# A sandwich transformer on one core: the third stage's ways laid out on a table with one hop between engines for each round

## What is computed

```python
# L2 attention: 16 heads of 8 channels, causal softmax over the 256 tokens, out projection
# L2 MLP
h = gelu(x @ w1 + b1, approximate=False); return h @ w2 + b2
# L3
xm = resid_mix_m[0] * x + resid_mix_m[1] * x0
vg = rms_norm(xm) @ in_proj_w; value, gate = vg[..., :256], vg[..., 256:]
value = silu(causal_conv(value, conv_w, 4) + conv_b)
y = selective_scan(value, A, xm @ B_proj_w, xm @ C_proj_w, dt, 64) + D_param * value
xm = xm + mamba_scale * (y * silu(gate) @ out_proj_w)
xm = xm + m_mlp_scale * mlp(rms_norm(xm), m_fc_w, m_proj_w)      # mlp: square(relu(n @ fc)) @ proj
xa = resid_mix_a[0] * xm + resid_mix_a[1] * x0
q, k, v = rms_norm(xa) @ q_w, ... @ k_w, ... @ v_w                # 16 heads, 4 key heads, 8 channels
q, k = apply_rope(rms_norm(q), cos, sin) * q_gain, apply_rope(rms_norm(k), cos, sin)
xa = xa + attn_scale * (causal_softmax_attention(q, k, v) @ o_w)
xa = xa + a_mlp_scale * mlp(rms_norm(xa), a_fc_w, a_proj_w)
```

## Time and profile before

| what | us |
|---|---|
| median of 2 runs (4128.28 to 4131.64) | 4129.96 |
| the profiled execution | 4135.6 |
| its span, first to last instruction | 4134.0 |
| third stage in it (2059.5 to 3815.0) | 1755.5 |
| PE busy in the span | 3113.1 (75%) |
| DVE busy | 2393.2 (58%) |
| ACT busy | 1826.8 (44%) |
| POOL busy | 622.3 (15%) |
| mean granted clock of PE | 0.832 |

### The profile page before, as it was taken

How to read it: one execution, slowest core, us unless ns; L and a number is a source line. 1 busy time by engine, 2 the same in 40 slices (tenths; PEclk the granted TensorE clock), 3 DMA queues, 4 the chain that set the end, 5 groups by cost and what they waited for, 6 DMA issues and landing times.

```text
span 4134.0 us, 76115 instructions
## 1 busy us (share of the span) xinstructions
PE 3113.1 (75%) x31950; PEld 2440.1 (59%) x31950; DVE 2393.2 (58%) x6438; ACT 1826.8 (44%) x3876; POOL 622.3 (15%) x651
## 2 busy tenths in 40 slices
PE   6788887788887688787666785866878659466795
PEld 3566665466665577687544673755747548354465
DVE  4655555664555798989742655656456455533327
ACT  3555555456554777777412332422424224212322
POOL 1210011110101222222200113021010220300000
PEclk7888988889988789899856897988879879766797
DMA  2000000000000000000000000000000000000000
GB/s 79 1 1 1 1 2 1 1 1 1 1 1 37 11 8 6 9 6 4 11 1 1 1 2 0 2 1 1 3 1 2 1 1 2 1 1 30 12 1 21
DMA packets 13542, 27.99 MB, mean 7 GB/s; under 512 B 784, under 2 KB 9232, under 8 KB 12688
## 3 DMA queue, kind: packets, MB, share of 16 engines
q1 hardware_dynamic: 13200, 23.12, 1.6%
HBM read 21.02 MB, written 2.10 MB: 6 GB/s over the span
## 4 chain that ended last, share of the span: by engine, by line
PE 51%; DVE 32%; ACT 10%; POOL 3%; issue 3%; DMA 0%; SPq 0%; DVEq 0%; POOLq 0%; ACTq 0%
PE ps L374 6%; PE ps L383 5%; DVE LN L2000 4%; PE ps L436 4%; PE ps L348 3%; PE ps L1878 3%; PE ps L525 3%; PE ps L1358 3%; POOL wAB L1755 3%; DVE LN L541 3%; DVE RS L289 2%; DVE LN L2013 2%; ACT LN L320 2%; DVE LN L310 2%; PE ps L443 1%
## 5 line engine op out<-in xcount | busy, mean ns | idle before, releaser
L356 ACT COPY LN<-ps 128x512 f32<-128x512 f32 (+4 forms) x592 | 303.5, 546 | 883.1 <-PE ps L348 474.7
L335 POOL TENSOR_TENSOR RS<-RS,MISC 128x4 f32<-128x4 f32 x216 | 220.4, 1021 | 2144.3 <-DVE RS L301 1687.2
L348 PE MATMUL ps<-cons,LN 128*128 128x128 f32 x672 | 149.4, 369 | 458.9 <-DVE LN L308 183.1
L541 DVE TENSOR_REDUCE LN<-ps 128x6 f32<-128x768 f32 x256 | 244.3, 956 | 288.9 <-PE ps L426 148.8
L348 PEld LDWEIGHTS ps<-cons,LN 128*128 128x128 f32 x672 | 103.2, 186 | 490.8 <-DVE LN L308 191.0
L436 PE MATMUL ps<-LN 32*128 32x256 f32 x1024 | 209.5, 488 | 105.1 <-DVE LN L541 39.6
L374 PE MATMUL ps<-LN,wAB 128*128 128x512 f32 x384 | 229.0, 727 | 16.9 <-ACT LN L393 8.5
L2000 DVE TENSOR_TENSOR LN<-LN 128x1024 f32<-128x1024 f32 (+2 forms) x192 | 220.3, 1147 | 27.8 <-ACT LN L356 16.9
L439 PE MATMUL ps<-LN 32*128 32x256 f32 x1024 | 210.1, 491 | 26.4 <-DVE LN L541 23.4
L687 DVE TENSOR_REDUCE M<-ps 128x12 f32<-128x1536 f32 x64 | 112.4, 1756 | 175.0 <-PE ps L426 174.9
L1878 PE MATMUL ps<-LN,wAB 128*128 128x128 f32 x1024 | 150.9, 310 | 74.2 <-ACT LN L356 73.7
(11 more groups left out here) (352 smaller groups left out, 7860.1 us busy)
## 6 DMA issues: line engine op xcount, KB each, us to landing
wAB<-wb SPq DMA_DIRECT2D x16, 256.0 KB, 2.7
LN<-wd SPq DMA_DIRECT2D x8, 512.0 KB, 6.7
...
```

The source lines that it names most:

```text
L335: pool.e.tensor_tensor(c.r[:, 40:44], c.r[:, 36:40], mhalf, ALU.pow).then_inc(*c.G.inc((k, "rstd")))
L348: ins = pe.e.transpose(ps[:, n * 128:(n + 1) * 128], src[:, n, :], ident)
L356: act.e.copy(dst, ps).then_inc(*c.A.inc(named(k, done)))
L541: return dve.e.tensor_reduce(cols[:, 2 - 2 * h:4 - 2 * h, :, q.at], src, X_AX, ALU.max, negate=True)
```

## The change

The parts of a lane's way get a table of rounds. A new class `Pace` counts rounds, and `p.to(n)` yields until round n; all engines of a part use the same numbers. Each step of DVE, POOL, PE and ACT gets a round of its own, so that what one engine makes in a round another takes in the next one. `mid` goes from 53 to 68 rounds (20 ahead of the scan, 32 in it, 16 behind), `l3_out` from 6 to 11, `l2_in` from 4 to 5, and couple 1 starts in round 60, not 52. A couple then has 8 + 50 + 71 + 50 + 19 + 50 + 71 + 50 + 14 = 383 rounds, and the stage 443. `dve_norm` is split (`dve_apply`), `dve_residual` applies a norm and adds, `pe_up` and `pe_down` are the two halves of `pe_mlp`. The instructions, their shapes and their number are the same, apart from the activation table loads, which follow the order of ACT's functions: there are 4 more of them in the third stage. The scan's own code and `attend` are not touched.

```diff
 LW = 8192
-LAG3, START3 = 3, (0, 52)
-ROUNDS3 = {"l2_in": 4, "mid": 53, "l3_out": 6}
+LAG3, START3 = 3, (0, 60)
+ROUNDS3 = {"l2_in": 5, "mid": 68, "l3_out": 11}
 START1 = (0, 4, 9, 13)
...
+
+    def __init__(self):
+        self.now = 0
+
+    def to(self, rnd):
+        while self.now < rnd:
+            self.now += 1
+            yield
...
         def pe_mid(pe, c, g):
-            v, attended = views23(c), couple_signals[c.n // 2][1]
+            v, attended, p = views23(c), couple_signals[c.n // 2][1], Pace()
             XT = v["XT"]
             k = (("l2", g // 4), c.n)
             pe.wait_ge(attended, (("l2", g // 4), 2 * (c.n % 2) + 1, "on"))
             pe_tok(pe, c, k, wv("l2o"), XT, 0, c.A, "y")
-            yield
-            yield
+            yield from p.to(5)
             k = (g, "l2f")
             pe.wait_ge(c.D, (k, "normed", 3))
             pe_tr4(pe, c, k, v["XN"], 0, c.A)
-            yield
+            yield from p.to(6)
             pe.wait_ge(c.A, (k, "xT"))
-            yield from pe_mlp(pe, c, k, XT, wv("l2w1"), 4, w3("l2w2"), v["h3"], c.D, c.A)
-            yield
-            yield
+            pe_up(pe, c, k, XT, wv("l2w1"), (0, 1), c.A)
+            yield from p.to(7)
+            pe_up(pe, c, k, XT, wv("l2w1"), (2, 3), c.A)
+            yield from p.to(8)
+            pe_down(pe, c, k, w3("l2w2"), v["h3"], c.A)
+            yield from p.to(13)
             k = (g, "l3m")
             pe.wait_ge(c.D, (k, "mixed"))
             pe_tr4(pe, c, k, v["Z"], 0, c.A)
-            yield
...
                         *c.P.inc((k, part, n)))
-                yield
+                yield from p.to(17 if part == "val" else 20)
             for b in range(2):
                 yield from pe_scan(pe, c, (g, "scan", b), b, v, (g, "l3n"), (g, "l3m"))
-            yield from pe_relu_mlp(pe, c, (g, "mm"), v, "mfc", "mpj")
-            yield
+            p.now = 52
+            yield from pe_relu_mlp(pe, c, (g, "mm"), v, "mfc", "mpj", p)
+            yield from p.to(61)
             k = (("l3", g // 4), c.n)
...
                 ins.then_inc(*c.P.inc((k, g2, "qkv_pe")))
-            yield
-            yield
-            yield
+            yield from p.to(67)
             pe.wait_ge(c.D, (k, "roped"))
             pe_tr4(pe, c, k, v["QK"][:, :, 0:128], 0, c.D, "qa")
             pe_tr4(pe, c, k, v["KR"], 1, c.A, "ka")
...
+        def pe_up(pe, c, k, xT, w1, js, by):
+            for j in js:
+                ps = c.bank(pe, j % 2, by, (k, "h", j))
+                pe.e.matmul(ps[:, :], w1[:, j * 128:(j + 1) * 128], xT, start=True, stop=True).then_inc(
+                    *c.P.inc((k, "up", j)))
+
+        def pe_down(pe, c, k, w2, h3, by):
...
+        def pe_relu_mlp(pe, c, k, v, fc, pj, p):
+            r = p.now
+            yield from p.to(r + 2)
             pe.wait_ge(c.D, (k, "normed", 3))
             pe_tr4(pe, c, k, v["YN"], 0, c.A)
-            yield
+            yield from p.to(r + 3)
...
             pe.wait_ge(c.A, (k, "xT"))
-            yield from pe_mlp(pe, c, k, v["XT"], wv(fc), 4, w3(pj), v["h3"], c.D, c.D)
+            pe_up(pe, c, k, v["XT"], wv(fc), (0, 1), c.D)
+            yield from p.to(r + 4)
+            pe_up(pe, c, k, v["XT"], wv(fc), (2, 3), c.D)
+            yield from p.to(r + 5)
+            pe_down(pe, c, k, w3(pj), v["h3"], c.D)

...
+        def dve_relu_mlp(dve, c, k, v, rep, p):
+            r = p.now
+            dve_stats(dve, c, k, v["Z"], rms=True, eps=EPS)
+            yield from p.to(r + 1)
+            dve_apply(dve, c, k, v["Z"], v["YN"], rms=True)
+            for i in range(2):
+                yield from p.to(r + 3 + i)
+                for j in (2 * i, 2 * i + 1):
+                    dve.wait_ge(c.A, (k, "relu", j))
+                    dve.e.scalar_tensor_tensor(v["h3"][:, j, :], c.ps[j % 2][:, :], 0.0, v["h3"][:, j, :], ALU.max,
+                                               ALU.mult).then_inc(*c.D.inc((k, "h", j)))
+            yield from p.to(r + 6)
             scaled(dve, c, k, "sum", "y", v["Z"], rep, v["tmp"])
...
         def dve_mid(dve, c, g):
-            v = views23(c)
+            v, p = views23(c), Pace()
             X, XN, O4, Z, YN, QK = XG[g], v["XN"], v["O4"], v["Z"], v["YN"], v["QK"]
-            k = (("l2", g // 4), c.n)
-            dve.wait_ge(c.A, (k, "y"))
-            yield from dve_post(dve, c, (g, "l2ap"), X, O4)
+            yield from p.to(1)
+            dve.wait_ge(c.A, ((("l2", g // 4), c.n), "y"))
+            dve_stats(dve, c, (g, "l2ap"), O4)
+            yield from p.to(2)
+            dve_residual(dve, c, (g, "l2ap"), X, O4)
+            yield from p.to(3)
+            dve_stats(dve, c, (g, "l2f"), X)
+            yield from p.to(4)
+            dve_apply(dve, c, (g, "l2f"), X, XN)
+            yield from p.to(9)
             k = (g, "l2f")
-            yield from dve_norm(dve, c, k, X, XN)
-            yield
-            yield
-            yield
             dve.wait_dma(got_ve)
             dve.wait_ge(c.P, (k, "sum"))
             dve.e.tensor_tensor(O4, v4(c.ps[0]), rep4(wv("l2b2")), ALU.add).then_inc(*c.D.inc((k, "y")))
-            yield from dve_post(dve, c, (g, "l2fp"), X, O4)
-            yield from dve_norm(dve, c, (g, "l3x"), X, XN)
+            dve_stats(dve, c, (g, "l2fp"), O4)
+            yield from p.to(10)
+            dve_residual(dve, c, (g, "l2fp"), X, O4)
+            yield from p.to(11)
+            dve_stats(dve, c, (g, "l3x"), X)
+            yield from p.to(12)
+            dve_apply(dve, c, (g, "l3x"), X, XN)
             dve.wait_ge(c.D)
             dve.wait_ge(DD[LANES], "rm")
             dve.e.tensor_tensor(Z, XN, rep4(wv("rm0")), ALU.mult).then_inc(*c.D.inc(((g, "l3m"), "mixed")))
+            yield from p.to(13)
             k = (g, "l3n")
-            yield from dve_norm(dve, c, k, Z, YN, rms=True, eps=EPS)
-            yield
+            dve_stats(dve, c, k, Z, rms=True, eps=EPS)
+            yield from p.to(14)
+            dve_apply(dve, c, k, Z, YN, rms=True)
             cw = wv("convw")
             for n in range(2):
+                yield from p.to(17 + n)
...
-                yield
+            yield from p.to(20)
             for b in range(2):
                 yield from dve_scan(dve, c, (g, "scan", b), b, v, k)
-            yield from dve_relu_mlp(dve, c, (g, "mm"), v, wv("mmsc"))
+            p.now = 52
+            yield from dve_relu_mlp(dve, c, (g, "mm"), v, wv("mmsc"), p)
             dve.wait_ge(c.D)
             mixed(dve, c, (g, "am"), Z, Z, wv("ra0"), XN, wv("ra1"), v["tmp"])
+            yield from p.to(59)
             k = (("l3", g // 4), c.n)
-            yield from dve_norm(dve, c, k, Z, YN, rms=True, eps=EPS)
-            yield
-            yield
+            dve_stats(dve, c, k, Z, rms=True, eps=EPS)
+            yield from p.to(60)
+            dve_apply(dve, c, k, Z, YN, rms=True)
+            yield from p.to(63)
             rb, sq, un = v["rb"], v["sq"], v["un"]
             dve.wait_ge(c.A, (k, 1, "qkv"))
...
-            yield
+            yield from p.to(64)
+            r4 = rb.rearrange("p (t c) -> p t c", c=20)
             dve.wait_ge(c.G, (k, "rms"))
...
         def dve_l3_out(dve, c, g):
-            v = views23(c)
+            v, p = views23(c), Pace()
+            yield from p.to(1)
             scaled(dve, c, (("l3", g // 4), c.n), "y_pe", "y", v["Z"], wv("asc"), v["tmp"])
-            yield from dve_relu_mlp(dve, c, (g, "am"), v, wv("amsc"))
-            yield from dve_post(dve, c, (g, "l3p"), XG[g], v["Z"])
-            yield
+            yield from p.to(2)
+            yield from dve_relu_mlp(dve, c, (g, "am"), v, wv("amsc"), p)
+            yield from p.to(9)
+            dve_stats(dve, c, (g, "l3p"), v["Z"])
+            yield from p.to(10)
+            dve_residual(dve, c, (g, "l3p"), XG[g], v["Z"])
+            yield from p.to(11)
...
+
+        def dve_residual(dve, c, k, X, Y):
+            dve_apply(dve, c, k, Y, Y)
+            dve.wait_ge(c.D)
+            dve.e.tensor_tensor(X, X, Y, ALU.add).then_inc(*c.D.inc((k, "x")))
```

More of the change, by code:

```diff
@@ L1740, in pool_mid @@
-            yield from pool_norm(pool, c, (g, "l3n"))
-            v = views23(c)
+            v, p = views23(c), Pace()
+            for r, name in ((1, "l2ap"), (3, "l2f"), (9, "l2fp"), (11, "l3x"), (13, "l3n")):
+                yield from p.to(r)
+                pool_rstd(pool, c, (g, name))
             pool.wait_ge(c.D, ((g, "l3m"), "mixed"))
             pool.e.memset(v["XV"], 0.0).then_inc(*c.G.inc((g, "scan", "zeros")))
-            yield from idle(3)
+            yield from p.to(20)
@@ L1760, in pool_l3_out @@
[L1760 to L1762 removed]
+            p = Pace()
+            yield from p.to(2)
+            pool_rstd(pool, c, (g, "am"))
+            yield from p.to(9)
+            pool_rstd(pool, c, (g, "l3p"))
+            yield from p.to(11)
         XTA, YA = LN[:, 0:4096], LN[:, 8192:12288].rearrange("p (b m e) -> p b m e", b=16, m=2)
```

165 lines of the change are left out of this document (83 added, 82 removed).

## The result

The changed kernel takes 4011.7 us (median of 2 runs, 4011.3 to 4012.1) where the kernel before took 4130.0: a ratio of 0.9714, 95% interval 0.9672 to 0.9755, 118 us or 2.9% faster. Its profiled span is 4009.8 us, 124 less than before. It lies in the forecast range (3945 to 4150) and on the forecast side; the forecast was 4066, so the gain was nearly twice the forecast one. It doesn't lie in the main case's own range (4020 to 4110), and the likeliest outcome by the chances was a difference of under 2% (0.56, against 0.38 for a gain of over 2%).

The account below looks back on a forecast made before the run. The prediction took scans as PE-bound and the third stage's rest as bound by waits. Rest 788 less 855.4, plus 4 elsewhere, gave -63.7 from 4135.6: 4071.9, or 4066 after the 5.6 median offset; range 3945 to 4150.

Parts of the forecast that it names:

- main case: Whole kernel: the summed forecast of 4066 us, chance 0.53, with its own range of 4020 to 4110.
- Bound: Third stage outside scans and attention alone: waits bind, no engine; PE's 350 us for normed input are all its idle time.
- the rest: Third stage's seven stretches with steps ahead of or behind the scan, `l3_out` or `l2_in`: from 855.4 to 788 us.
- Known stretches: Third stage's scans, attention beside attention, last attention and opening: priced by known rounds, together +4 us.
- The power: Head norms' power on POOL, 13.1 us, eight times: DVE's wait grows from 64.8 to 82 us, counted in full.
- The price of a round: 178 new rounds outside scans and attention alone: 706 us without the head norms' power, 4.0 each.
- packed rival: Same stretches: uneven rounds average out between queues, PE 87% busy, 659 us, total 3937; chance 0.25.
- The toll: Same stretches: each round costs its hops and loop whatever stands in it, 4.98 us, total 4166; chance 0.15.
- Table loads: ACT in the third stage: four more loads of 1.28 us, taken as nothing, 5 us kept for the range.
- It doesn't do what it says: Third stage: relu MLPs keep relu and square in one round, power one round long; little moves, 4110 to 4140; chance 0.07.

Follow-up runs that it names:

- the padded kernel: Kernel before with its old steps, empty rounds added to give each part its length after the change, couple 1 starting in round 60: 4191.3 us, ratio 1.0160.
- the kernel with the narrow power: Changed kernel with POOL's power of the head norms on 4 of its 80 columns, the other 76 left out: 3925.5 us, ratio 0.9495.

## Why the prediction came out as it did

**Bound.** That the rest is bound by waits and not by an engine was right: PE's waits for normed tiles fell from 350 to 127 us, and the padded kernel shows that separating the steps did it, not the rounds. That they were all of PE's idle time in the rest was read too simply. 32 of the 350 us stand in the opening, in both kernels; 317 of the 354 us of idle time in the rest were these waits, and some 95 of 245 are after the change.

**Known stretches.** Forecast +4 us in sum, measured -13.2 + 13.5 + 8.5 - 2.8 = +6.0. The sum is right in part by luck: attention beside attention took 7.5 us more than forecast (3.3 a round, not 3.1), and the opening was 4.9 us shorter because the stage began earlier.

**The power.** Forecast 82 us, in full on the path; measured 87.5 as a wait and 88 to 90 by taking it away. Right, with one thing not seen in it: POOL's queue holds the other norms, so that four more rounds to its use didn't hide it.

**The price of a round.** This is the term that was mis-sized: 706 us forecast for the 178 rounds without the power, 725.6 - 87.5 = 638 measured, 3.6 a round and not 4.0. The rounds ahead of the scan beside attention were right (4.1, measured 45.4 / 11 = 4.1; couple 1's attention begins at 2268.0 and 2997.1 in the two other stretches, which gives 3.9 and 4.0). The ten ahead of it beside `l2_in`, 2232.4 to 2268.0, took 3.6 and not 4.1, and the 19 with `l3_out` and `l2_in` of couple 1, 2932.8 to 2997.1, 3.4 and not 4.0. The rounds behind the scan beside attention were put at 3.6 and took 29.0 / 9 and 25.2 / 8, 3.2; `l3_out` and `l2_in` beside attention at 3.85, 31.2 / 9 = 3.5; and the 42 rounds in which both couples have steps at 4.6. Of these a half's 21 took 63.7 + 62.4 us with 44 us of power in them, 82 or 3.9 each: 14.5 us under the forecast, or 29 of the 68 us if the other half is taken alike. I see two errors in it, and no run tested either by itself. I put the floor of a round at the 2.9 us of a lone attention at the granted 0.57; in the short rounds behind the scan the clock was 0.93. And I took the larger of two sums for every round, and half a microsecond more for a hop, where light and heavy rounds even out between the queues: DVE was busy 67% of the rest. The second is what the packed rival argued. The rest came half of the way to this rival (62 of the 129 us from 788 to 659), and its sign showed in part: PE's busy time in the rest dropped from 501 to 480 us, at a clock of 0.85 in the last stretch. That the total stayed inside the range is due to the rivals in it; the main case with its own range missed.

**The toll.** Put at 5.0 us a round, 0.15. 50 empty rounds and the later start together cost 1.3 us a round, and the rest took 4.1 a round with the power in it; so a price of 4.8 or more is refuted.

**Table loads.** Taken as nothing, with 5 us as a bound. ACT's other order has them, and in the kernel with the power on ACT, which has some 18 table loads more in the stage than the changed kernel, the total is within 4 us of the kernel with the narrow power. So many loads cost nothing that these intervals can tell. By the Trainium skill, page "ScalarE: Activation LUTs", section "What ACT_TABLE_LOAD costs", each load would bring a drain of some 1380 ns; in the rows of the power on ACT the load at 2474.18 ends at 2475.46 and its activation starts at 2475.47, so the trace doesn't agree.

**It doesn't do what it says.** Not so for the whole: the time moved by 118 us. For the relu MLPs in part: the chain stayed in its round, and PE waits for squares, 74 us with the power and 35 without it, while DVE's waits fell from 61.1 to 16.8. Laying it out brought 9 to 14 us, within the intervals both times.

**The start.** I let the later start pass as a part of the table, without a price of its own. It cost 51 us in the changed kernel (11 with the power on ACT and the longer relu MLPs), and a median on the side of the forecast hid an edit that went the other way.
